# Flamingo-style gated block on one core: v's first projection placed behind the transposes of x1, the next scores ahead of it

## The reference

```
x1  = x  + tanh(g_xattn) * attention(layernorm(x), ctx)
out = x1 + tanh(g_ffn)   * hyper(layernorm(x1))
```

## Time and profile before

| | |
|---|---|
| median of 3 runs | 1775.77 us |
| lowest and highest | 1771.59 and 1778.42 us |
| the profiled execution | 1780.68 us, its span 1778.9 us |
| busy TensorE / VectorE / ScalarE / GpSimd | 1412.3 / 1288.7 / 1143.7 / 807.7 us |
| mean granted clock of TensorE | 0.924 of full speed |

### The profile page before, as it was taken

One profiled execution on the slowest core, in us unless ns is written; L12 is line 12 of the kernel. 1 busy time (PEld: TensorE's weight loads), 2 busy tenths in 40 slices (PEclk: granted clock), 3 DMA queues, 4 the chain that ended last, 5 costly groups with the idle time before them and its releaser, 6 DMA issues.

```text
span 1778.9 us, 36533 instructions
## 1 busy us (share of the span) xinstructions
PE 1412.3 (79%) x12644; PEld 890.2 (50%) x12800; DVE 1288.7 (72%) x3526; ACT 1143.7 (64%) x2337; POOL 807.7 (45%) x1373
## 2 busy tenths in 40 slices
PE   1769999988888988888888889888888897427735
PEld 0446566555554555554555455555555565224424
DVE  3334434566678888888788888887787778767988
ACT  2457877777677777776677667777677766423312
POOL 3323335355645563656555564556455644440000
PEclk9889999999999999998999999999999998768878
DMA  8557776666666767676677757676566544422123
GB/s 247 155 150 206 186 192 182 184 173 173 186 176 198 204 176 198 198 196 190 166 206 199 203 153 206 196 192 168 171 171 180 145 120 128 107 83 95 71 71 142
DMA packets 175464, 299.95 MB, mean 169 GB/s; under 512 B 25104, under 2 KB 76176, under 8 KB 171184
## 3 DMA queue, kind: packets, MB, share of 16 engines
q1 hardware_dynamic: 157872, 264.04, 49.5%
q0 software_dynamic: 17408, 33.56, 11.0%
HBM read 179.81 MB, written 67.11 MB: 139 GB/s over the span
## 4 chain that ended last, share of the span: by engine, by line
DVE 30%; PE 25%; ACT 14%; POOL 13%; issue 13%; SPq 3%; DMA 2%; DVEq 0%; POOLq 0%; ACTq 0%
PE pr L693 8%; PE pr L707 7%; POOL kp L583 7%; DVE ssum L1326 5%; ACT squares L998 3%; DVE sv L1327 3%; DVE xpre L1343 2%; POOL x1c L518 2%; DVE otile_even L1355 2%; DVE otile_even L1372 2%; DVE x1c L1222 2%; DVE sa L1327 2%; DVE negm L1204 2%; DVE otile_odd L1355 2%; ACT g_sb L976 2%
## 5 line engine op out<-in xcount | busy, mean ns | idle before, releaser
L583 POOL TENSOR_TENSOR kp<-ke,sv 128x64 f32<-128x64 f32 x329 | 149.3, 454 | 281.6 <-DVE sv L1327 280.9
L1326 DVE TENSOR_REDUCE ssum<-kp 128x16 f32<-128x64 f32 x768 | 182.2, 237 | 124.7 <-POOL kp L583 117.9
L499 POOL TENSOR_TENSOR x_hl<-xc,x_hl 128x512 bf16<-128x512 f32 x128 | 156.4, 1222 | 153.2 <-ACT x_hl L926 153.1
L707 PE MATMUL pr<-wv,ctx_hl 128*128 128x256 bf16 x1536 | 199.7, 292 | 29.4 <-DVE k_hl L1189 22.6
L583 POOL TENSOR_TENSOR kp<-ke,sa 128x64 f32<-128x64 f32 x343 | 149.7, 436 | 143.1 <-DVE sa L1327 143.0
L1212 DVE TENSOR_TENSOR o_sb<-av_ps,rden 128x128 f32<-128x128 f32 x256 | 72.7, 284 | 192.7 <-ACT rden L967 189.2
L1204 DVE TENSOR_REDUCE negm<-s_ps 128x4 bf16<-128x512 f32 x256 | 166.7, 651 | 61.3 <-PE s_ps L813 60.9
L840 PE MATMUL av_ps<-probs,v_t 128*32 128x128 f32 x2048 | 112.0, 289 | 124.0 <-DVE o_sb L1212 123.7
L693 PE MATMUL pr<-x_hl,wq 128*128 128x512 bf16 x707 | 171.5, 387 | 43.2 <-POOL x_hl L499 36.5
L693 PE MATMUL pr<-x_hl,wk 128*128 128x512 bf16 x736 | 195.3, 421 | 5.9 <-issue 4.5
L958 ACT ACTIVATE probs<-st_ps,key_bias 128x512 f32<-128x512 f32 x256 | 173.6, 678 | 36.9 <-PE st_ps L827 36.6
(11 more groups left out here) (171 smaller groups left out, 3096.4 us busy)
## 6 DMA issues: line engine op xcount, KB each, us to landing
xs<-in_dram SPq DMA_DIRECT2D x128, 256.0 KB, 5.7
xc<-in_dram SPq DMA_DIRECT2D x128, 256.0 KB, 4.3
ctx_raw<-in_dram SPq DMA_DIRECT2D x32, 1024.0 KB, 7.4
x1c<-in_dram POOLq DMA_DIRECT2D x64, 512.0 KB, 7.5
x_dram<-x1c SPq DMA_DIRECT2D x32, 1024.0 KB, 5.2
q_st<-q_hl SPq DMA_DIRECT2D x384, 64.0 KB
k_st<-k_hl SPq DMA_DIRECT2D x384, 64.0 KB
x1t_even<-x_dram SPq DMA_DIRECT2D x16, 1024.0 KB, 5.9
```

Of the source, the lines that this page charges most:

```text
L499: nc.gpsimd.tensor_tensor(x_hl[:, G % 2, 1, t, :], xc[:, t, :], x_hl[:, G % 2, 0, t, :], ALU.subtract).then_inc(x_split, 1)
L583: nc.gpsimd.tensor_tensor(kp[:], ke[:], v, ALU.mult).then_inc(kp_made, 1)
L707: ins = nc.tensor.matmul(bank(what)[:, j * E:(j + 1) * E], ctx_hl[:, a, t, win], wv[:, m, t, :], start=(t == 0 and a + m == 0), stop=(t == ...
L1326: cf.link(nc.vector.tensor_reduce(s_t, k, AX.X, ALU.add))
```

## The change

In step 4 v0 moves from the first place of the list behind the transposes t2 and t3. The scores of the next unit, which stand behind the first item, thereby stand behind t2. Nothing is computed in another way. In chunks without transposed parts in step 4 (0 and 1, and the one before chunk 0) v0 stays alone in the list; so the order differs in 29 chunks, 2 to 30.

```diff
@@ -140,10 +140,12 @@
     if 0 <= G + 1 < NG:
         made += {0: [("q", G + 1, 0)], 1: [("q", G + 1, 1)], 2: [("k", G + 1, 0)], 3: [("k", G + 1, 1)],
-                 4: [("v", G + 1, 0)], 7: [("v", G + 1, 1)]}.get(r, [])
+                 7: [("v", G + 1, 1)]}.get(r, [])
     if 0 <= G - 1 < NG and r in (5, 6):
         made += [("o", G - 1, 2 * (r - 5)), ("o", G - 1, 2 * (r - 5) + 1)]
     made += [("t", H, j) for H, j in at_step(g, 2, T_AT)]
+    if r == 4 and 0 <= G + 1 < NG:
+        made.append(("v", G + 1, 0))
     made += [("lg", H, 0) for H, j in at_step(g, 2, [LOGITS_AT])]
```

## The result

The changed kernel takes 1778.2 us in the median (1770.43 to 1782.12, 15 runs). The kernel before, now also with 15 runs, takes 1771.1 us (1764.19 to 1778.42). The ratio is 1.0035, with a 95% interval of 1.0022 to 1.0048: 6.2 us slower by the ratio (3.9 to 8.5); the two medians lie 7.1 apart. I had predicted +4.1 us and, from the 1775.77 of three runs, 1779.9. That 1778.2 comes so close to 1779.9 is in part luck: the kernel before turned out 4.7 us faster than those three runs had it, and the change costs some 2 us more than I said. The 6.2 us are within the 0.5% that I called no change, and with 15 runs it is none the less clear of zero.

What follows compares the result with a forecast made beforehand. The prediction took ScalarE's start of the squares in step 4 as the bound. Its terms, 5.0 (chunks 2 to 9) + 0 (10 to 30) - 0.9 (earlier scores) = +4.1 us, took 1775.77 to 1779.9 us, range 1767 to 1796.

Steps and rivals of the forecast that it cites:

- no change: The outcome of a measured time within about 0.5%, or 8.9 us, of the kernel before; given a chance of 0.61.
- What bounds step 4: In step 4, when ScalarE can begin the squares decides, 4.70 us ahead of VectorE's division; not when VectorE gets its scores.
- the six whose division does not wait for ScalarE: Chunks 9, 13, 17, 21, 25 and 29: the division of step 5 does not wait for ScalarE; in 23 others it does.
- Chunks 2, 3, 4, 6 and 8 at +0.50: In step 4, t3 waits for VectorE's low half of k1, so the squares start 0.50 us later; 2.5 us together.
- Chunks 7 and 9 at +1.23: In step 4, v0 had started before the maximum; with t3 waiting for k1 the squares start 1.23 us later; 2.5 together.
- Chunk 5 at +0.05: With the clock at half level in v0, k1 is read before t3 comes; cost 0 to 0.50 us, taken as 0.05.
- the clock rival: TensorE's clock falls more often in chunks with `pre`; up to 20 us slower, 1800 us; chance 0.22.
- Chunks 10 to 30 at 0: In step 4, t2 takes over v0's wait for k1 and the squares start unchanged; cost 0, 2 us either way.
- The credit of -0.9 for the earlier scores: In five chunks of the Sinkhorn stretch, earlier scores let the division go up to 0.38 us earlier: 0 to -1.9, half taken.
- my sign of being wrong: Across the kernel, the number of stretches at half clock changes by more than three.
- t3's wait costs nothing: Rival: in chunks 2 to 9 TensorE regains the 0.5 and 1.2 us in the next steps; 1774.9 us; chance 0.15.
- the earlier scores pay in full: Rival: VectorE's Sinkhorn work bounds, so the waits of 15 maxima of step 5 go, 10.4 us: 1765.4; chance 0.13.

Runs made afterwards that it cites:

- the exchanged banks: The changed kernel with t3 and v0 exchanging banks in chunks 2 to 9, so that v0 waits for k1; 1.0008 to the kernel before.
- the squares alone: The kernel before with the three squares of step 4 ahead of v0's copy on ScalarE; ratio 0.9771, median 1733.44 us.
- the first and third experiments: First: new order in chunks 2 to 9 alone, 1.0034. Third: changed kernel, t3 and v0 exchanging banks in chunks 2 to 9, 1.0008. Both to the kernel before.
- the second: The new order in chunks 10 to 30 alone, chunks 2 to 9 as in the kernel before; 0.9991 to the kernel before.
- the first experiment: The new order in chunks 2 to 9 alone, chunks 10 to 30 as in the kernel before; 1.0034 to the kernel before.

## Why the prediction was right, point by point

- **What bounds step 4** was read rightly: not the scores that VectorE waits for, but ScalarE's start of the squares. Moved by +0.5 us it cost 0.5 us a chunk; moved into ScalarE's wait for v0 it brought 41 us. But I had only one of the two paths from the squares to the division, the one over the reciprocal. In chunk 9, which I counted among the six whose division does not wait for ScalarE, it starts 0.04 us behind the end of the reciprocal; VectorE had idled just before, for GpSimd, which itself waited for the squares. So the 1.23 us that I charged to chunk 9 came true although my own count spoke against it.
- **Chunks 2, 3, 4, 6 and 8 at +0.50:** measured +0.5 each (36.9 to 37.4, 41.9 to 42.4, 40.1 to 40.6), and the exchanged banks take it away. **Chunks 7 and 9 at +1.23:** measured +1.3 each (39.9 to 41.2, 41.3 to 42.6); of chunk 7's, 0.5 goes with the bank, 0.8 stays with the maximum.
- **Chunk 5 at +0.05** was wrong for a reason that I had put into the clock rival. The stretch at half clock that lay in its v0 before isn't there in the changed kernel: 38.5 to 37.4. Against the 36.9 of chunks 2 to 4 it has the same +0.5 as they. So the eight chunks lose 5.6 us like for like, and 4.0 in these two profiles. Every profile of the old order early has a chunk longer by 1.5 to 1.7 us somewhere in 2 to 9 (5, 2 or 6, and the squares alone both 5 and 6). The three of the new order with its own banks have none, the two with exchanged banks have it in chunk 6. I can't say whether that is chance.
- **Chunks 10 to 30 at 0:** borne out within the intervals. The whole change costs 6.2 us and its early part alone 6.0; the late part alone measured -1.6, with zero well inside (-6.6 to +3.4).
- **The credit of -0.9 for the earlier scores** isn't visible, and its reason was wrong. I took it that in five chunks like 17 the division could come 0.38 us earlier if its maximum did, since the reciprocal was ready. But there the division stands behind GpSimd's wait for the squares (the rows of chunk 17 above), which earlier scores do not shorten. Without it the sum is +5.0, nearer to the +6.2 measured. The remaining 1.2 us lie within the interval (3.9 to 8.5).
- **The clock rival** fell. In the changed kernel v0 ran slow at least in part in 7 of the 29 chunks; before it was 10 (I had counted nine, which are those with `pre`; chunk 5 is the tenth). The granted clock is at its lower level in 25 stretches of chunks 2 to 30, and was in 27, so my sign of being wrong, a change by more than three, did not come. t2, t3 and the scores stand behind 1.85 us of idle in chunk 13, and v0 behind them ran at full clock; the mean clock between 960 and 1480 us is 0.96, and was 0.95. The Trainium skill ("TensorE: Matmul & The Clock Gate", Part 4) says that a transpose doesn't count as busy time as other products do. The 1800 us that I had set beside that rule did not come, but no run here has transposes without dense products close by, so the rule itself is neither borne out nor refuted. The window of the changed kernel:

```profile
960.00:1480.00 520.00, 450.49 (x4210) 282.56 (x4264) 427.35 (x1156) 375.68 (x767) 288.42 (x493) 0.96 0.66 177
```

- **"t3's wait costs nothing"** fell with the first and third experiments; **"the earlier scores pay in full"** with the second, whose interval begins at 0.9963.

## What to carry to other kernels

A list that hands out buffers in turn ties order and waiting together: move an item, and another inherits the wait that the long item had covered. Write down for each item which earlier reader it waits for, before and after, and when that reader ends. And where an engine waits in order for something late, look at what stands behind it: here three squares that needed nothing of v0 stood behind its copy, and putting them ahead was worth 41 us, while the order on TensorE was worth 6 the other way. Ask also who else waits for what is late: GpSimd did, and an engine that shows no wait for it at the place you look at (here VectorE at its division) may have waited for it one step earlier, through another engine.

## What the runs showed of the hardware

TensorE's clock adds a noise that a single profile can't see through. With identical instructions, chunks 10 to 30 took 1011.5 us in the profile of before and 1006.0 in that of the first experiment, in steps of 1 to 3 us in single chunks, and these go with where the stretches at half clock fell (chunk 15: 46.7 us without one, 49.3 us with). And the start up to chunk 2 varied from 150.2 to 153.7 us. An effect of 6 us had to be read from chunks with equal clock, not from spans.
